# A state-space mixer on one core: the tokens' second projection replaced by a copy and a shifting transfer

## What is computed

```
x      = u @ w_in_x.T                       # 256 wide, "tokens"
beta   = (1 - tr_t) * dt_t * alpha ; gamma = tr_t * dt_t
base   = B_t * (x[t-1] * beta + x[t] * gamma)
state  = state * alpha + rotated(base) ;  y[t] = C_t . state + D * x[t]
```

## Time and profile before

| | |
|---|---|
| median of three runs | 699.77 us |
| profiled execution, its time | 701.77 us |
| span of the profiled execution | 700.0 us |
| PE busy | 610.4 us (87%) |
| DVE busy | 495.2 us (71%) |
| ACT busy | 256.6 us (37%) |
| POOL busy | 261.2 us (37%) |
| mean granted TensorE clock | 0.947 of full speed |

### The profile page before, as it was taken

The page is one execution under the profiler, slowest core; times in us unless marked ns, Lnnn a source line. Parts: engine busy times, 40 slices in busy tenths (PEclk is TensorE's granted clock), DMA queues, the critical chain, the costliest instruction groups (busy, mean ns, idle before and its releaser), DMA issues. The chain is left out here.

```text
span 700.0 us, 17981 instructions
## 1 busy us (share of the span) xinstructions
PE 610.4 (87%) x6368; PEld 502.8 (72%) x6368; DVE 495.2 (71%) x1246; ACT 256.6 (37%) x444; POOL 261.2 (37%) x301
## 2 busy tenths in 40 slices
PE   6589999999999754888779879779799999999995
PEld 5467778778777553676667767557688888888884
DVE  2877887887887554657567667486578778787873
ACT  2443442443343200635445435335322323332221
POOL 4263754754752575405145144362101101110111
PEclk9989999999999975789999999999999999999998
DMA  6020000000000485275484763800001000000000
GB/s 204 0 62 1 16 15 0 15 15 14 1 16 1 114 200 99 70 142 133 106 159 126 138 132 93 188 6 6 32 0 32 30 0 30 30 0 30 16 16 16
DMA packets 53553, 40.34 MB, mean 58 GB/s; under 512 B 3968, under 2 KB 48288, under 8 KB 53488
## 3 DMA queue, kind: packets, MB, share of 16 engines
q1 hardware_dynamic: 50896, 36.74, 22.2%
q0 software_dynamic: 704, 1.92, 1.2%
q10 hardware_dynamic: 1888, 0.79, 0.6%
HBM read 24.10 MB, written 11.93 MB: 51 GB/s over the span
## 5 line engine op out<-in xcount | busy, mean ns | idle before, releaser
L1917 PE MATMUL bank<-xT_hl_c,w_up 128*128 128x512 f32 x432 | 118.1, 409 | 2.4 <-ACTq L67 2.4
L1244 DVE TENSOR_REDUCE nmax<-bank 128x4 f32<-128x512 f32 x112 | 72.0, 685 | 54.9 <-PE bank L1399 48.3
L141 POOL TENSOR_TENSOR rstd<-mv,norm_c 128x4 f32<-128x4 f32 x24 | 6.4, 267 | 264.3 <-DVE mv L135 251.2
L1151 ACT ACTIVATE prob<-bank 128x512 f32<-128x512 f32 x128 | 69.4, 594 | 67.2 <-PE bank L1399 42.0
L1917 PEld LDWEIGHTS bank<-xT_hl_c,w_up 128*128 128x128 f32 x432 | 76.1, 189 | 15.9 <-ACTq L67 2.7
L1389 PE MATMUL bank<-neg_i,mask 64*128 64x256 bf16 x512 | 54.3, 292 | 36.4 <-issue 9.5
L1839 ACT ACTIVATE sg<-bank 128x512 f32<-128x512 f32 x72 | 43.0, 597 | 105.3 <-PE bank L1917 105.3
L1933 PEld LDWEIGHTS bank<-w_down,hid 128*128 128x128 f32 x576 | 74.4, 191 | 5.9 <-issue 0.5
L738 POOL TENSOR_TENSOR ramp<-upto,dec_hl 128x512 fp32r<-128x512 f32 x64 | 66.8, 1073 | 26.1 <-PE bank L866 26.1
L1933 PE MATMUL bank<-w_down,hid 128*128 128x128 f32 x576 | 75.6, 275 | 0.0
L1872 DVE TENSOR_TENSOR gu<-sg,bank 128x512 f32<-128x512 f32 x64 | 43.8, 685 | 21.5 <-PE bank L1917 10.5
(11 more groups left out here) (227 smaller groups left out, 1265.1 us busy)
## 6 DMA issues: line engine op xcount, KB each, us to landing
q_stack<-q_scratch SPq DMA_DIRECT2D x32, 192.0 KB, 5.4
k_scratch<-k_part SPq DMA_DIRECT2D x8, 384.0 KB, 3.2
q_scratch<-q_part SPq DMA_DIRECT2D x8, 384.0 KB, 2.7
k_stack<-k_scratch SPq DMA_DIRECT2D x32, 96.0 KB
x<-xT_in SPq DMA_DIRECT2D x8, 256.0 KB, 8.3
mask<-mask_in SPq DMA_DIRECT2D x8, 256.0 KB, 6.0
xres<-x_in SPq DMA_DIRECT2D x8, 256.0 KB, 2.8
q_scratch<-q_part SPq DMA_DIRECT2D x8, 256.0 KB, 3.1
```

The lines of the kernel that those rows point to most:

```text
L1151: act.activation(prob[:, b % 2, ORDER[n], :, :], (TT0, TT1)[n % 2][:, :], ACT.Exp, scale=XD ** -0.5)\
L1244: dve.tensor_reduce(nmax[:, b, 4 * u:4 * u + 4], (SS0, SS1)[n % 2][:, :].rearrange("p (i k) -> p i k", i=4), AX_X, ALU.max, negate=True).t ...
L1917: mm = pe.matmul(bank[:, :], w_up[:, which, a, c, :], xT_hl[par][:, v, :], start=(n == 0), stop=(n == 2))
```

## The change

The projection of the shifted tokens is dropped. TensorE projects the tokens of a sequence once, at the start of the scores of the sequence before it ("a sequence ahead"); `front` no longer projects. ScalarE copies the projection out of the bank (`copy_tokens`, into `x_tok`). SyncE then issues a transfer within SBUF that writes rows 0 to 126 of `x_tok` into rows 1 to 127 of `x_sh`, whose row 0 is zeroed once. VectorE multiplies `x_tok` by gamma straight into `w_tok`, `x_sh` by beta into `xg`, and adds. To make room in SBUF the tile `whole` now shares its memory with `trig`.

```diff
+            def shift(g, b):
+                sp.wait_ge(s_xe.sem, s_xe.at(g, b))
+                sp.sem_inc(sp_passed, 1)
+                sp.wait_ge(s_w.sem, s_w.at(g, 3 * b - 5))
+                sp.sem_inc(sp_passed, 1)
+                sp.dma_start(x_sh[1:P, b % 2, :], x_tok[0:P - 1, b % 2, :]).then_inc(s_shift[b % 2].sem, 16)
...
+            def copy_tokens(g, b):
+                act.wait_ge(s_xx.sem, s_xx.at(g, b))
+                act.wait_ge(s_w.sem, s_w.at(g, 3 * b - 6))
+                act.wait_ge(s_shift[b % 2].sem, s_shift[b % 2].at(g, b // 2 - 1))
+                act.activation(x_tok[:, b % 2, :], PX[:, 0:D_INNER], ACT.Copy).then_inc(s_xe.sem, 1)
...
             def inputs_of(g, b):
-                dve.wait_ge(s_xx.sem, s_xx.at(g, b))
...
+                dve.wait_ge(s_xe.sem, s_xe.at(g, b))
+                dve.wait_ge(s_y.sem, s_y.at(g, b - 2))
+                dve.tensor_tensor(heads(w_tok[:, b % 2, :]), heads(x_tok[:, b % 2, :]), of(gamma), ALU.mult).then_inc(s_w.sem, 1)
+                dve.wait_ge(s_shift[b % 2].sem, s_shift[b % 2].at(g, b // 2))
                 dve.wait_ge(s_w.sem, s_w.at(g, 3 * b - 1))
-                dve.tensor_tensor(heads(xg[:, 0, :]), heads(PX[:, 0:D_INNER]), of(gamma), ALU.mult).then_inc(s_w.sem, 1)
-                dve.tensor_tensor(heads(xg[:, 1, :]), heads(PX[:, D_INNER:]), of(beta), ALU.mult).then_inc(s_w.sem, 1)
+                dve.tensor_tensor(heads(xg[:, :]), heads(x_sh[:, b % 2, :]), of(beta), ALU.mult).then_inc(s_w.sem, 1)
                 dve.wait_ge(s_w.sem, s_w.at(g, 3 * b + 1))
-                dve.wait_ge(s_y.sem, s_y.at(g, b - 2))
-                dve.tensor_tensor(w_tok[:, b % 2, :], xg[:, 0, :], xg[:, 1, :], ALU.add).then_inc(s_w.sem, 1)
+                dve.tensor_tensor(w_tok[:, b % 2, :], w_tok[:, b % 2, :], xg[:, :], ALU.add).then_inc(s_w.sem, 1)
...
-                pe.wait_ge(s_w.sem, s_w.at(g, 3 * b - 2))
-                tokens(par, b, 0)
...
+            def tokens(g, par, b):
+                pe.wait_ge(s_xe.sem, s_xe.at(g, b - 1))
                 for n, (a, v) in enumerate(((0, 0), (0, 1), (1, 0))):
-                    mm = pe.matmul(PX[:, shift * D_INNER:(shift + 1) * D_INNER], xhl[:, par, a, b, 1 - shift:P + 1 - shift],
-                                   w_x[:, v, :], start=(n == 0), stop=(n == 2))
-                return mm
-
-            def scores(g, par, b):
-                tokens(par, b, 1).then_inc(s_xx.sem, 1)
+                    mm = pe.matmul(PX[:, 0:D_INNER], xhl[:, par, a, b, 1:], w_x[:, v, :], start=(n == 0), stop=(n == 2))
+                mm.then_inc(s_xx.sem, 1)
+
+            def scores(g, par, b, left):
+                if b < GS - 1:
+                    tokens(g, par, b + 1)
+                elif left:
+                    pe.wait_ge(s_lo.sem, s_lo.at(g + 1))
+                    tokens(g + 1, 1 - par, 0)
```

## The result

| | before | changed |
|---|---|---|
| time, median (lowest to highest) | 700.3 us (695.9 to 701.3), 4 runs | 743.4 us (737.8 to 748.4), 4 runs |
| span of the profiled execution | 700.0 us | 738.7 us |
| first `k_part` of the last group (end of the mixer) | 234.0 us | 276.8 us |
| from there to the end of the span | 466.0 us | 461.9 us |

The changed kernel takes 1.062 times as long (95% interval 1.055 to 1.069). The sign was forecast, the size was not: 43 us slower instead of 11, and outside the range. All of it lies in the mixer: 42.8 us more up to `k_part` at 276.78, where the earlier trace rows has 233.96, and nothing more behind it.

A forecast was written before the change was run, and what follows sets the result against it. TensorE's path was taken to bound the mixer, with VectorE taking over after the change. Losses of 9.4 + 0.5 + 1.1 = +11.0 us, saved matmuls included, on the 699.8 us median gave 710.8 us, range 696 to 718.

The forecast's parts named there:

- What bounds the kernel: In the mixer, TensorE, busy 24.4 to 24.7 us of a group's 25.1 to 25.8, waiting mostly for GpSimd's ramp.
- the mechanism of the turns: Gamma and beta multiplications, now reading two SBUF tiles, alternate with GpSimd instructions, each waiting for the other's whole instruction.
- the walk: Step-by-step timing of a mixer group: four groups +1.3 us each, two +2.1; as walked 706 to 717 us, chance 0.61.
- This one has half that, I take 2.3 (bounds 1.5 and 4): Landing time of the SBUF shift in us, taken from a 256 KB row within SBUF that lands in 2.3.
- I take 0.5: First group: sequence 0's shift starts after the gates, costs VectorE 1 to 2 us, mostly covered; 0.5 us counted.
- The rival of a late transfer (0.05): Shift taking over 5.5 us outlasts VectorE's request for sequence 2; each us beyond costs one per group; 720 at 7 us.
- The sizes in the walk: Mixer losses: 9.4 us over groups 1 to 6, 0.5 at the start, 1.1 in the last group; sum +11.0 us.
- the likeliest case: VectorE and GpSimd alternate in the mixer at every step as timed: 706 to 717 us, chance 0.61.
- The rival of half the turns (0.24): Back-to-back VectorE instructions keep their turn; inputs(1) loses 0.9 us instead of 2.75; about 697 us (694 to 705), chance 0.24.
- ScalarE's copies: 32 added 256-wide copies on ScalarE, 0.4 us each, four a group, covered by its idle time.
- That is the whole gross gain: Three token matmuls fewer per sequence on TensorE, 0.45 us a set, 22 sets on the path: 9.9 us.
- What would show it wrong: Signs against the forecast: multiplications of 0.42 us beside busy GpSimd, VectorE waiting for the transfer, groups under 25 us.

The follow-up runs named there:

- inputs through ScalarE: Kernel before, both projections kept, but ScalarE copies the bank to SBUF and VectorE's gamma and beta multiplications read that copy: 713.3 us, ratio 1.019.
- the split kernel: Changed kernel with each 127-row transfer issued as two, of 112 and 15 rows, same bytes and result: 698.1 us.
- the repeated pair: Second traces, unedited, of the changed kernel and of the one with its transfer cut into 112 and 15 rows: 742.9 and 699.5 us.

## Why the prediction was wrong, point by point

- **What bounds the kernel, and the mechanism of the turns: right.** VectorE asked for sequence 2's shifted tokens 14.16 us after the residual sum (158.22 less the wait of 2.06, less 142.00), where the walk has 14.17 (135.45 less 121.28). mix(1) came at +9.10 us after the residual sum in the changed kernel, for +9.52 forecast. The means of gamma, beta and the add were 0.69, 0.75 and 0.77 us without the transfer. The Trainium skill's rule that was quoted (SBUF — State Buffer, "Who interferes with whom") is borne out by the inputs through ScalarE: the same two multiplications, with the source of the operands changed, mean 0.68 and 0.84 us where the one by gamma had 0.42.
- **"This one has half that, I take 2.3 (bounds 1.5 and 4)": this step failed.** It took 8.1 us, and 9.9 behind another. The row was near in kind and size, but not in shape: 128 partitions against 127. Size was taken as what matters. The bound of 4 was no bound either, since it came from the same row, and the same page has another transfer of this kind and size, under the attention's traffic, at a median of 6.8 us:

```profile
xs<-x SPq DMA_DIRECT2D x6, 256.0 KB, 6.8
```

The rest follows from it: for sequence 2 the transfer was due at 132 and the walk has VectorE ask at 135.45, a cover of about 3.5 us. A landing 5.8 us later than taken overruns that by some 2 us, and 2.06 was waited. This one step is worth 39.8 of the 42.8 us (276.8 less the split kernel's 237.0; 38.4 in the repeated pair).
- **"I take 0.5" for the start: failed with it.** The first residual sum came at 80.50 us, for 69.43 in the split kernel: 11.1 of the 39.8 us. Of that 5.9 lie at the first shift, for which VectorE waited 7.59 us (row below; 1.0 of the 5.9 is a later issue, 44.17 for 43.21, and the split kernel's repeat issued it at 44.07, so that part is chance); `theta` and `skip` could cover 1 to 2, not 8.
- **The rival of a late transfer (0.05)** named the right symptom and the right path: "over 5.5 us it outlasts the 135.45". Its price was too small. It was to cost one us a group for each us over 5.5, so 2.6 at 8.1. Measured, the six groups between the first and the seventh residual sum cost 28.6 us more than in the split kernel (184.3 for 155.7), 4.8 a group. The trace shows two things that the price left out: sequence 3's shift queues behind sequence 2's on the one DMA engine, so the group waits twice, and the granted clock falls in the stalls of TensorE (0.94 and 0.89 over two groups, with stretches at 0.50, for 1.00 before). How the 4.8 divides between them was not measured. Its reason was wrong too: it blamed the queue shared with `xres`, and `xres` was the victim.

The timeline of VectorE at the changed kernel's first shift, which was issued at 44.17:

```profile
52.32 0.42 DVE L839 TENSOR_TENSOR xg<-x_sh,beta 128x256 f32<-128x256 f32 x1 [7.59 <-DMA x_sh<-x_tok]
```

and in the split kernel, issued at 43.21:

```profile
46.46 0.43 DVE L840 TENSOR_TENSOR xg<-x_sh,beta 128x256 f32<-128x256 f32 x1 [1.75 <-DMA x_sh<-x_tok]
```

- **The sizes in the walk: too high.** At the mark, changed without transfer against before, +2.8 us was measured for +11.0 forecast. Start and group 0 gave -1.2 (forecast +0.5), groups 1 to 5 gave +3.2 (+8.1), group 6 +0.2 (+1.3), the last group up to `k_part` +0.5 (+1.1). In the group that I walked through +0.7 was left of +1.3. Elsewhere the second set of turns was not lost in full: in two of the groups of 25.2 us gamma ran in 0.41 to 0.42, and in those of 27.0 us gamma and beta both ran in 0.41, one behind the other, with only the add at 1.15, while one ramp instruction took 1.85. Who stands first at the lock changes from group to group, and the walk had VectorE second each time.
- **So a right transfer would not have made the forecast right.** With the transfer taken away or cut in two the kernel took 697.2 and 698.1 us: inside the range of 696 to 718 at its low end, but outside the 706 to 717 of the likeliest case. The rival of half the turns (0.24) said 697, and that it fits the time is luck: it had inputs(1) lose 0.9 us, and they lost 2.4 (mix(1) at 130.42 for 128.04).
- **ScalarE's copies: right.** 0.378 us each for 0.4, and hidden.
- **"That is the whole gross gain", 9.9 us for the saved matmuls: too high as well, as far as is known.** The fastest version here, which saves the same matmuls and has only the add in turns, as before, is 4.5 us ahead at the mark. Four of its six groups are shorter than the same groups before (two went from 25.1 to 23.9 us, two from 25.9 to 25.2), which those with the multiplications in turns were not. No run takes the matmuls away by themselves.
- **What would show it wrong** did: "VectorE waiting for the transfer" stands in the waits, 23.0 us in 15.

Not settled: why the part behind the mark differs by up to 10 us between kernels that share every instruction there but the last sequence's inputs. The three traces with two projections (before, its repeat, inputs through ScalarE) have 463.9 to 466.0 us, the ten with one projection 455.8 to 464.2, so a share of this may come with the change; the repeats show that a part is chance. The total times of the one-projection kernels look better than their marks for it: 697 to 698 for marks 3 us later than before. No experiment was aimed at it.

## What to carry to other kernels

Price a transfer by its shape before its size: count the rows of its outermost dimension, and if 16 does not divide them, look for a row of the trace with that very count, or cut the transfer into a multiple of 16 and a rest. A shift of a full tile by one partition makes 127 rows, the slowest count measured here. Where VectorE and GpSimd both read SBUF tiles, keep one operand in the bank, and do such work in VectorE's waits rather than ahead of instructions that will then meet GpSimd.

## What the runs showed of the hardware

- Within SBUF, rows of 1 KB: 112 rows land in 2.1 to 2.2 us, 15 rows in 2.0, 113 rows in 7.5, 127 rows in 8.1, and in 9.9 when one of the same kind is under way. One row more than 112 made this kernel 24 us slower. 127 rows of 512 bytes took 5.2 and 5.3.
- A transfer on a single DMA engine delays a broad one behind it: `xres`, 256 KB, 2.8 us before and 7.8 behind the shifts.
- In a stall of TensorE of 3.5 us the granted clock fell from 1.00 to 0.50 before TensorE had anything to do again, and then eight products took 1.12 us instead of 0.66.
- When VectorE instructions with two SBUF inputs meet GpSimd, the two mostly alternate at the end of each instruction: 1.26, 1.25 and 1.14 us for three VectorE instructions of 0.42, with GpSimd instructions of about 1.2 beside them. It is no strict order: in the groups of 27.0 us without the transfer two VectorE multiplications went through back to back (0.41 each) while a GpSimd instruction took 1.85.
